# The six scans of a batch in a sixteen-head attention kernel, placed at other units of VectorE's program

## What is computed

```python
scores = einsum('bhtd,bhsd->bhts', q, k) * scale      # 16 heads of width 16, causal
attn = softmax(scores)
seq_out = einsum('bhts,bhsd->bhtd', attn, v)
...
outer = Jw[..., :, None] * Jw[..., None, :]            # 6 x 6 per token and head
M_cumsum = cumsum(outer * decay_inv, axis=time)        # shifted by one token
M_all = M_cumsum * decay_fwd
rd_M = einsum('bhti,bhtij->bhtj', rd, M_all)           # then score_M, score_M2, a gate
```

## Time and profile before

| what | value |
|---|---|
| median of 3 runs | 918.17 us (914.5 to 918.22) |
| the profiled execution | 922.65 us, its span 920.9 us |
| PE busy | 760.2 us, 83% of the span |
| DVE busy | 625.1 us, 68% |
| POOL busy | 443.5 us, 48% |
| ACT busy | 353.1 us, 38% |
| mean granted PE clock | 0.896 |

### The profile page before, as it was taken

The page is one execution under the profiler, slowest core; times in us unless marked ns, Lnnn a source line. Parts: engine busy times, 40 slices in busy tenths (PEclk is TensorE's granted clock), DMA queues, the critical chain, the costliest instruction groups (busy, mean ns, idle before and its releaser), DMA issues.

```text
span 920.9 us, 12521 instructions
## 1 busy us (share of the span) xinstructions
PE 760.2 (83%) x4052; PEld 516.1 (56%) x4052; DVE 625.1 (68%) x2122; ACT 353.1 (38%) x709; POOL 443.5 (48%) x347
## 2 busy tenths in 40 slices
PE   6577553878988989989899886787799999899895
PEld 3343431545555656555455553455587778777774
DVE  2116453866886878868779689863576776776775
ACT  2210421444554545646446442553232332332420
POOL 9100643865653654637545464153553652662620
PEclk9887685989997989999999995677999999999998
DMA  8996369347464664656553732602022023022001
GB/s 291 189 216 113 78 91 138 55 86 166 78 153 95 110 143 72 149 106 130 130 88 87 145 73 40 186 5 92 1 69 92 1 93 92 0 93 92 24 1 46
DMA packets 60561, 90.01 MB, mean 98 GB/s; under 512 B 8248, under 2 KB 37456, under 8 KB 60496
## 3 DMA queue, kind: packets, MB, share of 16 engines
q1 hardware_dynamic: 60496, 89.22, 43.8%
HBM read 54.85 MB, written 33.82 MB: 96 GB/s over the span
## 4 chain that ended last, share of the span: by engine, by line
PE 37%; DVE 25%; POOL 12%; DMA 12%; issue 6%; SPq 4%; ACT 4%; ACTq 0%; POOLq 0%; DVEq 0%
PE ps L1236 11%; DVE ps L462 7%; PE ps L335 7%; PE ps L371 6%; DMA Q<-MT 6%; PE ps L324 5%; DVE Ob L510 4%; PE ps L312 4%; DMA qk_scratch<-HL 3%; SPq L673 2%; POOL MA L1142 2%; POOL MA L1154 2%; DMA Wm<-mem_scratch 2%; POOL OT L1170 2%; POOL XA L1143 2%
## 5 line engine op out<-in xcount | busy, mean ns | idle before, releaser
L462 DVE CUSTOM_DVE_ANT_0 ps<-ps,mask 128x256 f32<-128x256 f32 (+3 forms) x512 | 238.3, 508 | 86.6 <-PE ps L312 86.3
L405 ACT ACTIVATE Pr<-ps 128x512 f32<-128x512 f32 (+2 forms) x384 | 189.8, 527 | 149.2 <-PE ps L324 142.9
L324 PE MATMUL ps<-Q,K 98*128 98x256 f32 (+2 forms) x512 | 180.3, 395 | 55.5 <-DMA Q<-MT 43.7
L648 POOL TENSOR_SCALAR_AFFINE_SELECT Pr<-Pr 128x512 f32<-128x512 f32 x128 | 84.8, 667 | 219.9 <-ACT Pr L405 218.5
L312 PE MATMUL ps<-K,Q 96*128 96x256 f32 (+2 forms) x512 | 163.5, 365 | 30.5 <-DVE nmax L462 29.3
L1236 PE MATMUL ps<-ew_hi,XT 128*128 128x512 f32 x512 | 178.1, 409 | 0.0
L324 PEld LDWEIGHTS ps<-Q,K 98*128 98x128 f32 x512 | 97.8, 207 | 139.2 <-ACT Pr L405 56.6
L1360 DVE SCALAR_TENSOR_TENSOR A<-ps,cw,A 128x256 f32<-128x256 f32 x256 | 123.6, 483 | 58.7 <-PE ps L1236 47.2
L312 PEld LDWEIGHTS ps<-K,Q 96*128 96x128 f32 x512 | 106.2, 214 | 51.2 <-DVE nmax L462 42.4
L335 PE MATMUL ps<-Pr,V 128*17 128x512 f32 (+3 forms) x1024 | 106.1, 491 | 8.5 <-POOL Pr L648 8.5
L1236 PEld LDWEIGHTS ps<-ew_hi,XT 128*128 128x128 f32 x512 | 99.2, 194 | 20.9
(11 more groups left out here) (177 smaller groups left out, 1141.4 us busy)
## 6 DMA issues: line engine op xcount, KB each, us to landing
qk_scratch<-HL SPq DMA_DIRECT2D x32, 512.0 KB, 3.3
Q<-qk_scratch SPq DMA_DIRECT2D x96, 128.0 KB, 4.2
K<-qk_scratch SPq DMA_DIRECT2D x96, 128.0 KB, 5.7
Pr<-xT SPq DMA_DIRECT2D x8, 512.0 KB, 9.0
xraw<-xT SPq DMA_DIRECT2D x8, 512.0 KB, 6.3
mem_scratch<-Rl SPq DMA_DIRECT2D x16, 256.0 KB, 6.9
mv_scratch<-MV SPq DMA_DIRECT2D x32, 128.0 KB, 1.7
Wm<-mem_scratch SPq DMA_DIRECT2D x16, 256.0 KB, 10.4
```

The lines of the kernel that those rows point to most:

```text
L324: last = nc.tensor.matmul(o, K[0:STACK + 2, hh, P * kt:P * kt + P], Q[0:STACK + 2, hh, T - n:T], start=True, stop=True)
L405: nc.scalar.activation(probs(g % 2, kt, heads[0], len(heads)), src, ACT.Exp, scale=SCALE).then_inc(s_exp, 1)
L462: last = nc.vector.tensor_tensor_reduce(out=scores, in0=scores, in1=mask[:, T - w:T], scale=1.0, scalar=NEG, op0=ALU.add, op1=ALU.max, acc ...
L648: nc.gpsimd.affine_select(out=diagonal, in_=diagonal, compare_op=ALU.is_ge, fill=0.0, base=0, pattern=[[0, GROUP], [1, P]], channel_multip ...
```

## The change

One line: the units at which the six scans of a batch stand on DVE. The first half's scans stood at units 6, 8 and 10 of group 0, and stand at units 4 and 10 of group 0 and unit 4 of group 1; the second half's stood at the same units of group 2, and stand at units 4 and 10 of group 2 and unit 4 of group 3.

```diff
-        SCAN_AT = [(0, 6), (0, 8), (0, 10), (2, 6), (2, 8), (2, 10)]
+        SCAN_AT = [(0, 4), (0, 10), (1, 4), (2, 4), (2, 10), (3, 4)]
```

## The result

The change takes 926.21 us (median of 4 runs, 924.76 to 929.55) against 916.34 of the kernel before (914.48 to 918.22): ratio 1.0122, 95% interval 1.009 to 1.0153. Forecast were 925, with a range of 911 to 933, and slower. The same kernel measured again (experiment 9) gave 1.0062 (1.003 to 1.0093). So there is a loss, 9.9 us between the medians the first time and 4.8 the second; its size isn't settled more closely than that. Its profiled execution took 926.77 us, the span 925.0.

The account below looks back on a forecast made before the run. DVE was taken to set the pace from unit 5 to 11 of groups 0 and 2, PE's pace being 12.57 us. Gain -21.4, POOL +17.5, clock +10, end +1 sum to +7.1 us: 925 against the 918.17 median, range 911 to 933.

Parts of the forecast that it names:

- The gain from two scans less in groups 0 and 2: Both stretches shrink to PE's pace of 12.57 us: 3.57 us per batch, 21.4 us over six batches.
- DVE has room for it: In groups 0 and 2, DVE with one scan has some 11.8 us of work for PE's 12.57 us.
- The scans at unit 4 cost nothing where they can start: A 1.13 us scan fits DVE's idle of 1.15 to 3.97 us ahead of the mark, if started at once.
- the mark: The start of DVE's first row maximum of unit 5 in each group, used as the ruler for stretch times.
- POOL late: Group 3 to 0: POOL's masks and L856 run late, delaying DVE's scan and the mark 3.5 us, five times: 17.5 us.
- The split of x: DVE work slowing L856 to 4.36 us from 3.45; lateness is 2.2 us if nobody pays for it, 3.5 was taken.
- A scan beside a mask: The scan at (0, 4) starts with POOL's first mask of group 0: some 0.4 us more, at most 0.63.
- The clock: PE's idle of 2 to 2.5 us at unit 6 lowers its clock: 2.0 us a time, five times, 10 us.
- The scans of the first half, hidden by the wait for MT: In group 1 the mask is late too, but PE's MT wait hides it, at no cost.
- Group 1 to 2 unchanged: PE's wait for MT in group 1, 2.6 us a time on average, stays; no term in the sum.
- The end: After batch 6 POOL's lateness meets the start of batch 7: 1 us, between 0 and 2.2.
- The rival in which MT's wait shrinks: HL is written sooner, so loads of Q and K clear MT's way in group 1: 907 us, chance 0.05.

Follow-up runs that it names:

- experiment 9: The change itself measured once more, against the kernel before: 924.65 us, ratio 1.0062.
- Experiment 5: The change with the two scans of unit 10 in groups 0 and 2 moved to unit 9: 909.14 us, ratio 0.9907.
- Experiments 1 and 2: The change with its first scan at (0, 6): 914.76 us; the change with second-half scans at (2, 4), (2, 8), (2, 10): 908.97 us.
- Experiment 4: The change with nine unread matmuls ahead of the transpose of the maxima in group 0, batches 2 to 6: 921.2 us, ratio 1.0019.
- experiments 5 and 6: The change with both scans of unit 10 moved to unit 9: 909.14 us; the change with only group 0's moved there: 916.72 us.

## Why the prediction was right

- *The gain from two scans less in groups 0 and 2, forecast 21.4 us:* too large. With the clock at 1.00 the stretches took 13.29 and 13.15 us, not 12.57, so 6 x 1.17 + 6 x 1.10 = 13.6. The step that failed is "DVE has room for it", by which I held a sum of busy time, 11.8 us, against 12.57. The sum is right (11.80 in the window above), but DVE can't use all of the time: it stands 0.76 us for the transposed output and then has the rest in one piece. Experiment 5 moved a scan into that gap and got 12.55.
- *The scans at unit 4 cost nothing where they can start:* right. The idle time ahead of the mark fell to 0.54 us in groups 2 and 3 and to 0.28 in group 1, and no mark was held up by them.
- *POOL late, 3.5 us at the mark, 17.5 in all:* right, 3.30 and 16.5, in each batch from 2 to 6. By parts: the mask at unit 0 0.78 us late (0.9 forecast), DVE's wait 2.57 (3.1), PE's idle at unit 6 2.42 (2 to 2.5). The split of x was paid for by the masks, four in 3.38 us, as foreseen, and L856 had its 3.49 alone. Experiments 1 and 2 took away one end of this chain each, and with it 2.5 and 2.1 of the 3.3 us; what stayed is the mask at unit 0 in the one, a wait of 0.83 us in the other.
- *A scan beside a mask, some 0.4 us more and at most 0.63:* the lower value was right. The mask ended at 248.59 + 0.64 = 249.23 and the scan that was issued while it ran at 248.67 + 1.63 = 250.30, 1.07 us behind it; in the rows of experiment 5 it is 288.91 and 289.99, 1.08 behind it. The scan at (0, 4) took 1.63 us in all five batches, where one that begins beside no mask takes 1.21 to 1.22: 0.42 us more. The whole mask's 0.63, with 3.7 a time, was too much.
- *The clock, 10 us:* right in size. It fell in each of the five groups 0 (a mean of 0.78), for 2.1 us each, 10.5 in all, and in the second measurement 7.8. In the kernel before it fell behind each of the six waits for MT, to 0.50 for 3.41 us in four batches, 6.83 in batch 5 and 10.24 in batch 2. Experiment 4 showed that in group 0 it is the idle time and nothing else in the stretch: with some 0.1 us of it left the clock was 1.00.
- *The scans of the first half, hidden by the wait for MT:* right. POOL's L860 waits 6.4 us there, and no wait for a mask shows in group 1 to 2.
- *Group 1 to 2 unchanged:* not quite. MT was waited for as before, 2.77, 2.36, 2.27, 2.72, 2.98 and 2.68 us, but the clock fell for less long (1.00 in batch 1 and 0.90 in the others, before 0.75 to 0.90), -5.9 us. The executions of one kernel differ by as much here (913.58 to 925.83 us in 29 of the kernel before), so I count this as chance. That the sum came so close is luck. Against the forecast the parts were off by +7.8 (the gain), -5.9 (group 1 to 2), -1.5 (a fall of the clock that the kernel before had in group 0 of batch 3, 0.89, 15.98 us instead of 14.46, and that the forecast left out), -1.0 (POOL), +0.5 (the clock) and +0.4 (the end); together that is +0.3, from +7.1 to the marks' +7.4. Without the -5.9 the marks would have given +13, at the upper end of the range.
- *The end, 1 us:* 1.4.
- *The rival in which MT's wait shrinks* was given 0.05 because all transfers hang on the mark. For the change that held; but the ground was wrong, since the write of HL hangs on unit 11, not on the mark, and experiments 5 and 6 moved it.

## What to carry to other kernels

Where an engine is to do some work "beside" another's, look up both ends of it: who waits for its result, with everything that this engine has in its list ahead of its next delivery, and who hands over its input. Here the gap at unit 4 was real and the scans fitted in. But from one scan to the next, POOL's products and masks form a chain of 14.7 us, and DVE, with the mark behind the second scan in its list, was ready for that scan 2.5 us before the chain ended. And a sum of busy time below the period says only that work could fit; a timeline with its waits says whether it does.

## What the runs showed of the hardware

- The granted clock fell behind idles of PE that cost little themselves. I sorted the stretches from mark to mark of batches 1 to 6, in all thirteen profiles, by the longest idle of PE in them. The clock went from 1.00 to 0.50 for 3.4, 6.8 or 10.2 us beside or behind this idle in 69 of 78 with an idle of 2.05 to 3.3 us, in 8 of 17 with 1.3 to 2.0, in 3 of 12 with 1.1 to 1.2, in 7 of 33 with 0.95, and in none of 159 with less. Behind the same idle of 2.4 us in the same place a fall of 3.4 or 6.8 us made the stretch 0.7 to 2.3 us longer; the fall of 10.2 us in group 1 of batch 2 of the kernel before cost 4.9 by the prediction's estimate. With nine matmuls in that idle, whose result nobody reads, the clock was 1.00 in all five batches (experiment 4).
- A scan that was issued while a mask ran on POOL ended 1.07 to 1.08 us after the mask did, in the rows above; alone such a scan took 1.21 to 1.22 us, beside the masks of these rows 1.57 and 1.63. So it mattered here what was issued just ahead, not only how much work there was. On POOL, L856 took 4.36 us when issued within DVE's split of x, and 3.49 us outside it.
- A transfer of 8 KB landed 2.3 us after its issue in group 0 and kept PE waiting in group 1, 2.36 us in batch 2 of the change, where the loads of Q and K stand ahead of it; issuing those 0.9 us sooner brought the landing from 5.2 to 4.2 us behind the issue and shortened the wait by 1 us.
